# Strassen products for q, k and v in one phase, and attention that reads k and v from DRAM

## The chip, the core and the metric

The kernel runs on one core of one Trainium2 chip. The metric is device time in microseconds. Before the change three runs took 3925.47, 3927.17 and 3927.51 us; the median is 3927.17 us. The engines are TensorE (PE, with its weight loads listed apart as PEld), VectorE (DVE), ScalarE (ACT), GpSimd (POOL) and SyncE (SP), which here only issues DMAs.

## What is computed

A cross-attention block and a sparse feed-forward block, all in float32. There are 16 batches of 100 latent rows of 1024 numbers, and for each batch a context of 361 rows of 1024. There are 32 heads of 128 in 4 groups that share k and v.

```
x1  = x + xattn(layernorm(x), ctx, Wq, Wk, Wv, Wo)
out = x1 + ffn(layernorm(x1), c1_w, c2_w, w1, w2t)

xattn(latents, context):
    hidden = concat([context, latents], axis=1)      # 461 rows a batch
    q = latents @ Wq                                 # 32 heads of 128
    k = hidden @ Wk ; v = hidden @ Wv                # 4 groups of 128
    scores = q . k / sqrt(128)
    out = softmax(scores) . v
    return out @ Wo
```

Note that the context goes into k and v as it is, and the latents are normalised first.

## The kernel before

Every product is made to nearly float32 accuracy out of three matmuls. Each operand is split into a high part (ScalarE's copy into the type fp32r) and a low part (VectorE subtracts the high part from the original). `product` (line 21) then adds high x high, high x low and low x high for each chunk of 128 contraction rows; `PAIRS` lists the three. Its matmul is line 26, so several products of the kernel share that line and are told apart by their tiles.

The phases up to the first output projection are:

- `normalise` (line 45) reads x, normalises it and transposes it into `xt`, with its two parts.
- `project_queries` (line 203) runs over the 32 heads of Wq. For each head it makes 4 tiles of 400 columns, 24 matmuls each (8 chunks of three). It stores q to `q_scratch` in DRAM. Behind the heads it splits Wk and Wv into `wkv`, which stays in SBUF, and it saves `xt` to DRAM.
- `attend` (line 333) loops over the 16 batches. One batch has 4 groups of 800 query rows in tiles of 116 (7 tiles a group, 28 a batch). The tiles pass through a pipeline, written out by hand for each engine. In step i, PE makes the scores of tile i (`score`, three matmuls of 462 columns), then the piece of the weighing that is due (`weigh`, line 635), then the four transposes of tile i - 3 (`turn`, line 622). VectorE takes the row maximum, ScalarE the exponential and its sum, VectorE the reciprocal, GpSimd scales the probabilities (line 552), PE transposes them, ScalarE and VectorE make the two parts of `pt`. When half a group's columns (400) stand in `pt`, they are weighed with v in three pieces of four matmuls. GpSimd also splits q for the next group (lines 539 and 543).
- Between these steps PE also makes v of the same batch (line 599, six steps), transposes the context of the next batch (line 578) and makes the next batch's k (line 587). ScalarE and VectorE split each of the results (lines 690 and 722). These pieces are dealt to the steps by `v_work` and `k_work`.

A semaphore wait stands in front of each instruction that needs another engine's result, and each engine goes through its own list in order. So an instruction that waits holds back all that is behind it on its engine.

The rest (`project_out`, a second `normalise`, the gate, `hidden_layer`, a second `project_out`) isn't touched.

## Time and profile before

| what | value |
|---|---|
| median of three runs | 3927.17 us |
| the profiled execution, span of core 0 | 3928.4 us |
| PE busy | 3767.7 us, 96% |
| PE weight loads busy | 3331.3 us, 85% |
| VectorE busy | 1663.9 us, 42% |
| ScalarE busy | 1179.7 us, 30% |
| GpSimd busy | 534.1 us, 14% |
| mean granted clock of TensorE | 0.982 |
| last operation of attention ends | 2151.8 us |

The profile gives a span from the first to the last instruction; for this execution it has no other time. Busy time of PE is the time in which some matmul was under way. Matmuls overlap, so the mean duration of one is longer than the distance at which they follow each other; the distance is what counts, and it is read from counts in a stretch or from two start times. A number in square brackets behind a row is the idle time of the engine just ahead of it, with what ended it.

### The profile page before, as it was taken

The numbers are of one execution on the slowest core, as the hardware profiler recorded it, in microseconds if no ns is written. First come the engines' busy times: TensorE is split into PE (matmuls) and PEld (weight loads), VectorE is DVE, ScalarE is ACT, GpSimd is POOL, SyncE is SP. The second block draws the span as 40 slices with busy tenths as digits, with TensorE's granted clock in tenths as the row PEclk, the third lists the DMA queues.
The fourth block names the chain that finished last, engine by engine and source line by source line (L and its number), as shares of the span: only waits on it lengthen the run. The fifth ranks groups of instructions, "written<-read, shape, count | busy, mean of one in ns | idle before, by whom it ended". The sixth has DMA issues, their size and how long they took to land. (4 is left out here: it accounts for less than half of the span.)

```text
span 3928.4 us, 57189 instructions
## 1 busy us (share of the span) xinstructions
PE 3767.7 (96%) x19678; PEld 3331.3 (85%) x19678; DVE 1663.9 (42%) x2934; ACT 1179.7 (30%) x2353; POOL 534.1 (14%) x786
## 2 busy tenths in 40 slices
PE   6999998999999999999998999999699999899999
PEld 6999997888888888888887787787699999788787
DVE  4111112555555555555554432432565666332322
ACT  3111112444444444444444322322311111222321
POOL 0000000333333333333333100000000000000000
PEclk8999998999999999999999999999899999999999
DMA  4665554222222222222221644543211121444543
GB/s 120 125 126 95 78 80 108 59 67 57 57 57 63 59 57 57 61 61 57 57 57 53 183 123 118 182 123 100 85 69 68 56 74 61 135 129 128 173 124 102
DMA packets 469228, 357.91 MB, mean 91 GB/s; under 512 B 193328, under 2 KB 418608, under 8 KB 468144
## 3 DMA queue, kind: packets, MB, share of 16 engines
q1 hardware_dynamic: 463648, 330.03, 32.2%
q0 software_dynamic: 5520, 27.10, 1.9%
q8 instruction: 35, 0.57, 0.1%
q14 instruction: 25, 0.20, 0.0%
HBM read 255.49 MB, written 101.58 MB: 91 GB/s over the span
## 5 line engine op out<-in xcount | busy, mean ns | idle before, releaser
L1337 PE MATMUL wo_acc<-wo_w,wo_l 128*128 128x512 f32 (+1 forms) x2496 | 576.0, 393 | 23.2 <-DVE wo_l L1287 22.9
L1337 PEld LDWEIGHTS wo_acc<-wo_w,wo_l 128*128 128x128 f32 (+1 forms) x2496 | 461.8, 185 | 137.3 <-DVE wo_w L1311 23.1
L26 PE MATMUL q_acc<-xt,wq_parts 128*128 128x400 f32 x3072 | 560.6, 345 | 9.0 <-DVE wq_parts L307 9.0
L26 PEld LDWEIGHTS q_acc<-xt,wq_parts 128*128 128x128 f32 x3072 | 560.2, 188 | 9.2 <-issue 9.2
L1337 PE MATMUL w_acc<-w_w,w_l 128*128 128x512 f32 (+1 forms) x2184 | 503.6, 393 | 22.2 <-DVE w_l L1287 22.2
L26 PE MATMUL hid_acc<-x1t,hid_w 128*128 128x400 f32 x2688 | 508.7, 347 | 1.9 <-DVE hid_h L1100 1.4
L1337 PEld LDWEIGHTS w_acc<-w_w,w_l 128*128 128x128 f32 (+1 forms) x2184 | 405.1, 186 | 120.6 <-DVE w_w L1311 24.6
L26 PEld LDWEIGHTS hid_acc<-x1t,hid_w 128*128 128x128 f32 x2688 | 487.3, 189 | 2.6 <-issue 1.6
L552 POOL TENSOR_SCALAR probs<-probs,inverse 116x461 f32<-116x461 f32 (+1 forms) x448 | 293.4, 655 | 1025.9 <-DVE inverse L740 1025.4
L698 ACT ACTIVATE pt<-turned 128x464 fp32r<-128x464 f32 (+1 forms) x448 | 247.4, 552 | 582.0 <-PE turned L622 580.9
L732 DVE TENSOR_REDUCE negmax<-scores 116x1 f32<-116x461 f32 (+1 forms) x448 | 283.3, 632 | 311.4 <-PE scores L26 311.4
L587 PE MATMUL kvb<-hst,wkv 128*128 128x462 f32 x1536 | 387.4, 386 | 1.2 <-DVE hst L722 1.2
L599 PE MATMUL kvb<-wkv,hst 128*128 128x512 f32 (+1 forms) x1536 | 376.0, 397 | 0.0
L746 DVE TENSOR_TENSOR pt<-turned,pt 128x464 fp32r<-128x464 f32 (+1 forms) x448 | 283.0, 632 | 219.4 <-ACT pt L698 211.3
L26 PE MATMUL scores<-kt,q_parts 128*116 128x462 f32 (+1 forms) x1344 | 369.2, 383 | 2.3 <-DVE kt L722 1.5
L635 PE MATMUL outs<-pt,v 128*128 128x400 f32 (+1 forms) x1536 | 344.5, 346 | 7.6 <-DVE v L722 6.2
L599 PEld LDWEIGHTS kvb<-wkv,hst 128*128 128x128 f32 (+1 forms) x1536 | 269.9, 178 | 75.7
L705 ACT ACTIVATE probs<-scores,negmax 116x461 f32<-116x461 f32 (+1 forms) x448 | 288.4, 644 | 142.8 <-DVE negmax L732 140.7
L635 PEld LDWEIGHTS outs<-pt,v 128*128 128x128 f32 (+1 forms) x1536 | 283.4, 189 | 33.7 <-issue 11.8
L587 PEld LDWEIGHTS kvb<-hst,wkv 128*128 128x128 f32 x1536 | 275.5, 191 | 23.3 <-issue 1.5
L1287 DVE TENSOR_TENSOR wo_l<-wo_l_raw,wo_l 128x512 fp32r<-128x512 f32 (+1 forms) x208 | 139.3, 672 | 342.1 <-ACT wo_l L1260 342.1
L26 PEld LDWEIGHTS scores<-kt,q_parts 128*116 128x116 f32 (+1 forms) x1344 | 223.7, 178 | 39.9 <-issue 1.9
(98 smaller groups left out, 2926.7 us busy)
## 6 DMA issues: line engine op xcount, KB each, us to landing
wo_l_raw<-o_scratch SPq DMA_DIRECT2D x192, 256.0 KB, 2.8
w_l_raw<-h_scratch SPq DMA_DIRECT2D x168, 256.0 KB, 2.9
q_scratch<-q_stage SPq DMA_DIRECT2D x32, 800.0 KB, 8.2
q_raw<-q_scratch SPq DMA_DIRECT2D x64, 400.0 KB, 3.2
o_scratch<-o_stage SPq DMA_DIRECT2D x64, 400.0 KB, 3.9
h_scratch<-hid_h SPq DMA_DIRECT2D x28, 800.0 KB, 3.7
wq_raw<-in_L_xattn_Wq_dram SPq DMA_DIRECT2D x32, 512.0 KB, 8.1
ctx_raw<-in_ctx_dram SPq DMA_DIRECT2D x16, 1024.0 KB, 7.2
```

The costliest lines, as they stand in the source:

```text
L26: last = pe.matmul(out, left(a, c), right(b, c), start=(c == 0 and (a, b) == PAIRS[0]), stop=(c == chunks - 1 and (a, b) == PAIRS[-1]))
L552: pool.tensor_scalar(probs[:n, i % RB, :kv], probs[:n, i % RB, :kv], inverse[:n, i % RB:i % RB + 1], 1.0, ALU.mult, ALU.mult).then_inc(sca ...
L587: mm = pe.matmul(kvb[:, u % KB, :kvp], wkv[:, 0, a, c, g * P:(g + 1) * P], hst[:, e, c, :], start=(x == 0), stop=(x == products - 1))
L599: mm = pe.matmul(kvb[:n, k % KB, :], hst[:, a, c, at:at + n], wkv[:, 1, e, c, :], start=(x == 0), stop=(x == products - 1))
L635: mm = pe.matmul(outs[:, h, :half], v[:n, a, k, g * P:(g + 1) * P], pt[:n, e, k, h * half:(h + 1) * half], start=(x == 0), stop=(x == NC * ...
L698: act.activation(pt[:, 0, :, at:at + n], turned_tile(j, n), ACT.Copy).then_inc(pt_high, 1)
L705: act.activation(probs[:n, i % RB, :kv], scores[:n, i % SB, :kv], ACT.Exp, bias=negmax[:n, i % RB:i % RB + 1], accum_out=total[:n, i % RB: ...
L732: dve.tensor_reduce(negmax[:n, i % RB:i % RB + 1], scores[:n, i % SB, :kv], AX.X, ALU.max, negate=True).then_inc(s_max, 1)
L746: dve.tensor_tensor(pt[:, 1, :, at:at + n], turned_tile(j, n), pt[:, 0, :, at:at + n].bitcast(F32), ALU.subtract).then_inc(pt_low, 1)
L1287: dve.tensor_tensor(l[j % 2][:, 1, :, :rows], l_raw[j % 2][:, :, :rows], l[j % 2][:, 0, :, :rows].bitcast(F32), ALU.subtract).then_inc(l_l ...
L1337: last = pe.matmul(acc[p][:rows, :], l[j % 2][:, a, k, :rows], w[:, c, m * per + k, :], start=(m == 0 and k == 0 and (a, c) == PAIRS[0]), ...
```

## The change

`normalise` for x, `project_queries` and the k and v work inside `attend` are replaced by one function, `project`. It goes through ten sets of columns: eight of two batches of context (362 columns each, one of them padding), and two of eight batches of x (400 columns twice). For each set it goes through pairs of weight blocks: block n and the block half the heads away. A pair of weight blocks, a pair of column halves and the two halves of the 1024 contraction rows make a product of 2 x 2 blocks, and this is done by Strassen's scheme (in Winograd's form) with seven block products instead of eight. Each has 4 chunks of three matmuls. The sums of blocks that the scheme needs ahead are made by GpSimd (`sums_w` for every pair, `sums_x` and `last_x` for every set); ScalarE and VectorE split the seven results for each operand into parts; the sums behind the products are made out of PSUM by ScalarE (two copies) and VectorE (five). The tiles of the next set are transposed between the products of the present one. The parts of the next set's x operand (`high_x`, `low_x`) are made during the last pair of the set, each as soon as the product that reads the old one is done.

All of q, k and v are stored to DRAM. `attend` reads them from there: k comes as it is needed, v is transposed (line 877) since it is stored with its channels first. The tiles have 128 rows. Six fill 768 of a group's 800 rows, and the 32 rows that are left of each of the four groups make one tile more, the tail tile, the first of its batch. That gives 25 tiles a batch. Its 12 score matmuls take each group's k in turn, against a q that is zero elsewhere. GpSimd copies the tail's columns for group G to the end of `pt` (`bring_tail`, line 842) ahead of the second half's weighing. The halves have now 384 and 416 columns. A weighing now starts one step after the last transpose of its half (`s = j - step_of(...) - 1`). The score banks are three instead of two. Everything is unrolled: there are no hardware loops in either function.

On PE, in the last batch of before, around the end of a first half: `turned` are the transposed probabilities, `outs` the weighed sums. The first transpose here is of the half's last tile.

```order
L622 MATMUL turned<-ident,probs 128x116 [waits pt_low,scaled]
L622 MATMUL turned<-ident,probs 128x116 x3
L26 MATMUL scores<-kt,q_parts 116x462 [waits exped,q_split]
L26 MATMUL scores<-kt,q_parts 116x462 x2
L622 MATMUL turned<-ident,probs 128x116 [waits pt_low,scaled]
L622 MATMUL turned<-ident,probs 128x116 x3
L26 MATMUL scores<-kt,q_parts 116x462 [waits exped]
L26 MATMUL scores<-kt,q_parts 116x462 x2
L635 MATMUL outs<-pt,v 128x400 [waits o_out,pt_low]
L635 MATMUL outs<-pt,v 128x400 x3
```

After the change, in the first batch, at the end of a second half. The transpose of 128x128 is of the half's last tile.

```order
L26 MATMUL scores<-kt,q_parts 128x462 [waits exped]
L26 MATMUL scores<-kt,q_parts 128x462 x2
L925 MATMUL outs<-pt,v 128x384 x4
L906 MATMUL turned<-ident,probs 128x128 [waits pt_low,scaled]
L906 MATMUL turned<-ident,probs 128x128 x2
L906 MATMUL turned<-ident,probs 77x128
L26 MATMUL scores<-kt,q_parts 128x462 [waits exped]
L26 MATMUL scores<-kt,q_parts 128x462 x2
L925 MATMUL outs<-pt,v 128x416 [waits tail_in,pt_low]
L925 MATMUL outs<-pt,v 128x416 x3
```

One tile was transposed between the half's last tile and its weighing; now there is none, and the weighing waits on `tail_in` too.

On GpSimd, one group of before: the scaling of the probabilities with the pieces of q between.

```order
L552 TENSOR_SCALAR probs<-probs,inverse 116x461 [waits inverted] x2
L539 TENSOR_SCALAR q_parts<-q_raw 128x400 [waits q_landed1]
L552 TENSOR_SCALAR probs<-probs,inverse 116x461 [waits inverted]
L543 TENSOR_TENSOR q_parts<-q_raw,q_parts 128x400 [waits q_high]
L552 TENSOR_SCALAR probs<-probs,inverse 116x461 [waits inverted]
L539 TENSOR_SCALAR q_parts<-q_raw 128x400
L552 TENSOR_SCALAR probs<-probs,inverse 116x461 [waits inverted]
L543 TENSOR_TENSOR q_parts<-q_raw,q_parts 128x400 [waits q_high]
L552 TENSOR_SCALAR probs<-probs,inverse 116x461 [waits inverted]
L552 TENSOR_SCALAR probs<-probs,inverse 104x461 [waits inverted]
```

After the change, from the middle of group 0 of the first batch on: `kt` is the low part of the next batch's k, the COPY is `bring_tail`.

```order
L855 TENSOR_SCALAR probs<-probs,inverse 128x461 [waits inverted] x3
L812 TENSOR_SCALAR q_parts<-q_raw 128x384 [waits s_full,q_landed0]
L855 TENSOR_SCALAR probs<-probs,inverse 128x461 [waits inverted]
L812 TENSOR_SCALAR q_parts<-q_raw 128x384
L833 TENSOR_TENSOR kt<-k_raw,kt 128x462 [waits k_high]
L842 COPY pt<-pt_tail 128x8x32 [waits pt_low]
L855 TENSOR_SCALAR probs<-probs,inverse 128x461 [waits inverted]
L816 TENSOR_TENSOR q_parts<-q_raw,q_parts 128x384 [waits q_high]
L855 TENSOR_SCALAR probs<-probs,inverse 128x461 [waits inverted]
```

The low parts of k, which VectorE made before, and the copy of the tail's columns have come to GpSimd, and the copy stands behind a scaling, a piece of q and a part of k.

The diff, cut to its core:

```diff
-def project_queries(nc, sem, wq, kv_sources, wkv, xt, q_dram, xt_dram, scale, batches, rows, stage_free, saved):
+A, B, C, D = range(4)
+BANK = (A, B, A, D, B, C, D)
+def project(nc, sem, x, ctx, wq, wk, wv, ident, q_dram, k_dram, v_dram, scale):
...
+    sets = [("ctx", p) for p in range(NCTX)] + [("x", t) for t in range(batches // (2 * per))]
+    def pairs_of(s):
+        kv = [(kind, g) for kind in ("k", "v") for g in range(groups // 2)]
+        return kv if sets[s][0] == "ctx" else [("q", n) for n in range(heads // 2)] + kv
+    work = [(s, kind, n) for s in range(NS) for kind, n in pairs_of(s)]
+    NG = len(work)
+    opens = [min(g for g in range(NG) if work[g][0] == s) for s in range(NS)] + [NG]
...
+    def turn_slot(t):
+        s, k = tiles[t][0], t - of_set[tiles[t][0]][0]
+        if s == 0:
+            return -1
+        return 7 * opens[s - 1] + (2 + 2 * k if sets[s][0] == "ctx" else 3 + 2 * k if s == NCTX else 12 + 4 * k)
...
+        def w_from(G, i):
+            r = wr[G % 2]
+            return (r[:, 0, :half, :], sf[:, 1], r[:, 0, half:, :], sf[:, 0], sf[:, 2], r[:, 1, half:, :], sf[:, 3])[i]
...
+            def sums_w(G):
+                r = wr[G % 2]
+                pool.wait_ge(w_landed[G % 2], 32 * (G // 2 + 1))
+                if G:
+                    pool.wait_ge(s_made, 4 * G)
+                    pool.wait_ge(w_low, 7 * (G - 1) + 4)
+                pool.tensor_tensor(sf[:, 0], r[:, 1, :half, :], r[:, 1, half:, :], ALU.add).then_inc(s_made, 1)
+                pool.wait_ge(s_made, 4 * G + 1)
+                pool.tensor_tensor(sf[:, 1], sf[:, 0], r[:, 0, :half, :], ALU.subtract).then_inc(s_made, 1)
+                if G:
+                    pool.wait_ge(w_low, 7 * (G - 1) + 5)
+                pool.tensor_tensor(sf[:, 2], r[:, 0, :half, :], r[:, 1, :half, :], ALU.subtract).then_inc(s_made, 1)
+                if G:
+                    pool.wait_ge(w_low, 7 * (G - 1) + 7)
+                pool.wait_ge(s_made, 4 * G + 2)
+                pool.tensor_tensor(sf[:, 3], r[:, 0, half:, :], sf[:, 1], ALU.subtract).then_inc(s_made, 1)
+            def sums_x(s):
+                n = columns(s)
+                pool.wait_ge(xf_full, of_set[s][-1] + 1)
+                if s:
+                    pool.wait_ge(x_low, 7 * (s - 1) + 6)
+                pool.tensor_tensor(tf[:, 0, :, :n], xf[:, :half, 1, :n], xf[:, :half, 0, :n],
+                                   ALU.subtract).then_inc(t_made, 1)
+                pool.wait_ge(t_made, 4 * s + 1)
+                pool.tensor_tensor(tf[:, 1, :, :n], xf[:, half:, 1, :n], tf[:, 0, :, :n],
+                                   ALU.subtract).then_inc(t_made, 1)
+                pool.tensor_tensor(tf[:, 2, :, :n], xf[:, half:, 1, :n], xf[:, :half, 1, :n],
+                                   ALU.subtract).then_inc(t_made, 1)
+            def last_x(s):
+                n = columns(s)
+                pool.wait_ge(x_low, 7 * s + 2)
+                pool.tensor_tensor(tf[:, 1, :, :n], xf[:, half:, 0, :n], tf[:, 1, :, :n],
+                                   ALU.subtract).then_inc(t_made, 1)
...
+            for G in range(NG):
+                s = work[G][0]
+                if G + 1 < NG:
+                    sums_w(G + 1)
+                if s + 1 < NS:
+                    if G == ends[s] - 1:
+                        sums_x(s + 1)
+                    if G == ends[s]:
+                        last_x(s + 1)
...
+            for G in range(NG):
+                s = work[G][0]
+                n = columns(s)
+                for i in range(7):
+                    p = 7 * G + i
+                    pe.wait_ge(w_low, p + 1)
+                    if G == opens[s]:
+                        pe.wait_ge(x_low, 7 * s + i + 1)
+                    if i == 0 and G:
+                        pe.wait_ge(by_act, 2 * G)
+                    if i == 1 and G:
+                        pe.wait_ge(by_dve, 5 * (G - 1) + 2)
+                    if i == 2:
+                        pe.wait_ge(by_act, 2 * G + 1)
+                    if i == 3 and G:
+                        pe.wait_ge(by_dve, 5 * G)
+                    if i == 4:
+                        pe.wait_ge(by_dve, 5 * G + 1)
+                    if i == 6:
+                        pe.wait_ge(by_dve, 5 * G + 3)
+                    opened = i in (2, 4, 6)
+                    for c in range(half):
+                        for a, e in PAIRS:
+                            last = pe.matmul(bank[:, BANK[i], :n], wo[:, i, a, c, :], xo[:, i, e, c, :n],
+                                             start=(not opened and c == 0 and (a, e) == PAIRS[0]),
+                                             stop=(c == half - 1 and (a, e) == PAIRS[-1]),
+                                             skip_group_check=opened)
+                    last.then_inc(prod, 1)
+                    for t in turns[p]:
+                        turn(t)
...
+                for i in range(7):
+                    p = 7 * G + i
+                    if i == 1:
+                        dve.wait_ge(prod, p + 1)
+                        dve.wait_ge(by_act, 2 * G + 1)
+                        if G:
+                            dve.wait_ge(by_dve, 5 * G)
+                        add(G, u2, B, s1, n, f)
+                    if i == 4:
+                        dve.wait_ge(prod, p + 1)
+                        add(G, u3, B, s1, n, f)
+                        if G:
+                            dve.wait_ge(stored[3], 16 * G)
+                        dve.wait_ge(by_dve, 5 * G + 2)
+                        add(G, out[3], D, u3, n, f)
+                    if i == 5:
+                        dve.wait_ge(prod, p + 1)
+                        if G:
+                            dve.wait_ge(stored[2], 16 * G)
+                        add(G, out[2], C, u3, n, f)
+                    if i == 6:
+                        dve.wait_ge(prod, p + 1)
+                        if G:
+                            dve.wait_ge(stored[1], 16 * G)
+                        add(G, out[1], D, u2, n, f)
+                    if G + 1 < NG:
+                        low_w(G + 1, i)
+                    if G == ends[s] and s + 1 < NS:
+                        low_x(s + 1, i)
-def attend(nc, sem, ctx, xt_dram, q_dram, wkv, o_dram, ident, q_stored, xt_stored, o_free):
+def attend(nc, sem, q_dram, k_dram, v_dram, o_dram, ident, o_free):
...
+    TG = cols // P
+    body = TG * P
+    left = cols - body
+    split = body // 2
+    NT = 1 + groups * TG
+    N = batches * NT
+    NGR = batches * groups
+    SB, TB, OB, RB, LAG, PARTS = 3, 2, 2, 4, 3, 3
+    spans = ((0, split), (split, cols))
+    assert left * groups == P and NC * P <= 512
+    def place(I):
+        b, i = divmod(I, NT)
+        return (b, None, None) if i == 0 else (b, groups * b + (i - 1) // TG, (i - 1) % TG)
...
+    def pieces(j):
+        out = []
+        for G in range(max(0, groups * (j // NT) - 2), min(NGR, groups * (j // NT + 1))):
+            for h in range(2):
+                s = j - step_of(G, TG // 2 - 1 if h == 0 else TG - 1) - 1
+                if 0 <= s < PARTS:
+                    out.append((G, h, s))
+        return out
...
+            def low_k(b, g):
+                pool.wait_ge(k_high, groups * b + g + 1)
+                pool.tensor_tensor(kt[b % 2][:, 1, g], k_raw[:, g], kt[b % 2][:, 0, g].bitcast(F32),
+                                   ALU.subtract).then_inc(k_low, 1)
+            def bring_tail(G):
+                g = G % groups
+                pool.wait_ge(pt_low, (G // groups) * NT + 1)
+                if G:
+                    pool.wait_ge(o_full, 2 * G)
+                pool.tensor_copy(pt[:, :, :, body:], pt_tail[:, :, :, g * left:(g + 1) * left]).then_inc(tail_in, 1)
...
+            for I in range(N + LAG + 1):
+                if I < N:
+                    b, G, t = place(I)
+                    pool.wait_ge(inverted, I + 1)
+                    pool.tensor_scalar(probs[:, I % RB, :kv], probs[:, I % RB, :kv], inverse[:, I % RB:I % RB + 1],
+                                       1.0, ALU.mult, ALU.mult).then_inc(scaled, 1)
+                    if t is not None and 0 <= t < 4 and G + 1 < NGR:
+                        split_q(G + 1, *divmod(t, 2))
+                    if I % NT in (8, 10, 12, 14) and b + 1 < batches:
+                        low_k(b + 1, (I % NT - 8) // 2)
+                    if I % NT == 18 and b + 1 < batches:
+                        split_tail(b + 1)
+                j = I - LAG - 1
+                if j >= 0 and place(j)[2] == 3:
+                    bring_tail(place(j)[1])
...
+            def weigh(G, h, s):
+                b, g = divmod(G, groups)
+                lo, hi = spans[h]
+                for x in range(NC * len(PAIRS) * s // PARTS, NC * len(PAIRS) * (s + 1) // PARTS):
+                    k, (a, e) = x // len(PAIRS), PAIRS[x % len(PAIRS)]
+                    n = kv_chunks[k][1]
+                    if x == 0:
+                        pe.wait_ge(pt_low, step_of(G, TG // 2 - 1 if h == 0 else TG - 1) + 1)
+                        if h == 1:
+                            pe.wait_ge(tail_in, G + 1)
+                        if h == 0 and g == 0:
+                            pe.wait_ge(v_low, NC * (b + 1))
+                        if G:
+                            pe.wait_ge(o_act if h == 0 else o_dve, G)
+                    last = pe.matmul(outs[:, h, :hi - lo], v[b % 2][:n, a, k, g * P:(g + 1) * P], pt[:n, e, k, lo:hi],
...
+            for I in range(LAST):
+                if I < N:
+                    score(I)
+                j = I - LAG
+                for G, h, s in pieces(j) if j >= 0 else ():
+                    weigh(G, h, s)
+                if 0 <= j < N:
+                    turn(j)
+                b, i = divmod(I, NT)
+                if i in (8, 11, 14, 17) and b + 1 < batches:
+                    turn_v(b + 1, (i - 8) // 3)
...
-                normalise(nc, sem, "ln1", x.rearrange("b r n -> (b r) n"), xt, ident)
-                project_queries(nc, sem, wq, (wk, wv), wkv, xt, q_dram, xt_dram, float(d) ** -0.5, batches, rows,
-                                q_stored, xt_stored)
-            attend(nc, sem, ctx, xt_dram, q_dram, wkv, o_dram, ident, q_stored, xt_stored, o_stored)
+        project(nc, sem, x, ctx, wq, wk, wv, ident, q_dram, k_dram, v_dram, float(d) ** -0.5)
+        attend(nc, sem, q_dram, k_dram, v_dram, o_dram, ident, o_stored)
```

## Rows read from the trace of the kernel before

**Rows 1.** Windows by stage: from:to, length, busy us (count), PEclk, DMA share, GB/s
```profile
0.00:55.80 55.80, 21.12 (x104) 19.77 (x105) 36.60 (x81) 30.98 (x33) 1.10 (x8) 0.76 0.40 137
55.80:616.40 560.60, 560.60 (x3072) 560.23 (x3072) 83.75 (x102) 72.45 (x103) 4.43 (x8) 1.00 0.55 104
616.40:663.20 46.80, 28.58 (x122) 24.10 (x121) 7.41 (x13) 6.95 (x13) 4.93 (x6) 0.74 0.51 125
663.20:2078.10 1414.90, 1396.12 (x7620) 1204.68 (x7621) 737.78 (x1619) 623.93 (x1514) 455.66 (x660) 1.00 0.22 58
2078.10:2151.80 73.70, 70.59 (x389) 59.69 (x387) 42.45 (x97) 36.17 (x89) 27.31 (x40) 1.00 0.13 34
2151.80:3928.40 1776.60, 1690.73 (x8374) 1462.79 (x8374) 755.92 (x1023) 409.18 (x603) 40.69 (x64) 0.98 0.37 114
```

**Rows 2.** Windows, 100 us of the query phase
```profile
200.00:300.00 100.00, 100.00 (x552) 100.00 (x551) 12.50 (x17) 11.37 (x17) 1.60 (x3) 1.00 0.66 128
```

**Rows 3.** Timeline, last batch: start us, us, engine, line ... [idle <-releaser]
```profile
2113.57 0.56 PE L622 MATMUL turned<-ident,probs 116*128 116x116 f32 x4
2113.89 0.86 PE L26 MATMUL scores<-kt,q_parts 128*116 128x462 f32 x3
2114.16 0.56 ACT L698 ACTIVATE pt<-turned 128x464 fp32r<-128x464 f32 x1 [0.63 <-PE turned L622]
2114.59 0.90 PE L635 MATMUL outs<-pt,v 128*128 128x400 f32 x4
2114.75 0.64 DVE L746 TENSOR_TENSOR pt<-turned,pt 128x464 fp32r<-128x464 f32 x1 [0.61 <-ACT pt L698]
2115.33 0.56 PE L622 MATMUL turned<-ident,probs 116*128 116x116 f32 x4
```

**Rows 4.** Timeline, the end of the last batch
```profile
2141.72 0.86 PE L26 MATMUL scores<-kt,q_parts 128*104 128x462 f32 x3
2143.14 0.96 PE L622 MATMUL turned<-ident,probs 116*128 116x116 f32 x8
2143.74 0.56 ACT L698 ACTIVATE pt<-turned 128x464 fp32r<-128x464 f32 x1 [0.57 <-PE turned L622]
2144.04 0.65 POOL L552 TENSOR_SCALAR probs<-probs,inverse 116x461 f32<-116x461 f32 x1 [1.11 <-DVE inverse L740]
2144.33 0.64 DVE L746 TENSOR_TENSOR pt<-turned,pt 128x464 fp32r<-128x464 f32 x1 [0.49 <-ACT pt L698]
2145.03 1.00 PE L635 MATMUL outs<-pt,v 128*128 128x400 f32 x4 [0.93 <-DVE pt L746]
```

**Rows 5.** Groups by line and form: xcount | busy us, mean ns | idle
```profile
L543 POOL TENSOR_TENSOR q_parts<-q_raw,q_parts 128x400 fp32r<-128x400 f32 x128 | 134.5, 1051 | 0.2
L539 POOL TENSOR_SCALAR q_parts<-q_raw 128x400 fp32r<-128x400 f32 x128 | 67.3, 526 | 14.5 <-DMA q_raw<-q_scratch 14.5
L1287 DVE TENSOR_TENSOR wo_l<-wo_l_raw,wo_l 128x512 fp32r<-128x512 f32 x192 | 132.5, 692 | 308.7 <-ACT wo_l L1260 308.7
L307 DVE TENSOR_TENSOR wq_parts<-wq_raw,wq_parts 128x1024 fp32r<-128x1024 f32 x32 | 39.2, 1226 | 22.9 <-ACT wq_parts L278 22.9
L1100 DVE SCALAR_TENSOR_TENSOR hid_h<-hid_acc,hid_mask_t 128x400 f32<-128x400 f32 x112 | 59.0, 568 | 132.3 <-ACT hid_mask_t L1044 121.6 <-PE hid_acc L26 5.5 <-issue 5.2
```

**Rows 6.** Timeline of PE in the hidden layer
```profile
3060.84 0.60 PE L954 MATMUL turn<-ident,hid_raw 128*128 128x128 f32 x4
3061.20 0.72 PE L965 MATMUL gate<-c2s,zs 80*128 x4
3061.76 0.53 PE L26 MATMUL hid_acc<-x1t,hid_w 128*128 128x400 f32 x2
```

**Rows 7.** DMA queue, 400 to 500 us: packets, MB, share of 16 engines
```profile
q1 hardware_dynamic: 17250, 7.41, 47.3%
```

**Rows 8.** Timeline, the first transposes of attention
```profile
630.32 1.44 PE L578 MATMUL kvb<-ident,ctx_raw 128*128 128x128 f32 x6 [13.90 <-DMA ctx_raw<-in_ctx_dram]
```

**Rows 9.** Windows, 20 us of the first output projection
```profile
2180.00:2200.00 20.00, 16.38 (x65) 12.55 (x64) 11.74 (x13) 8.84 (x11) 0.00 (x0) 0.93 0.81 259
```

939 lines of the change are left out of this document (505 added, 434 removed).

## Prediction

> **What bounds the kernel now.** I read five views. First the stretches by stage [rows 1]: TensorE (PE) is busy for 560.6 of 560.6 us in the query phase, for 1396 of 1415 us in the attention loop and for 70.6 of 73.7 us in its last batch; nothing else passes 740 us in the loop. So up to 2151.8 us the end is set by the number of matmuls and by what each one takes. Second, the rate inside one line [rows 2]: 552 matmuls of 400 columns in 100 us, 181.2 ns each. Third, the last batch in order of time [rows 3, 4], the only stretch of before in which attention runs without k or v products between its steps: what an attention step takes there, and how long a tile needs from its transpose to the moment when it can be weighed. Fourth, the costs of single operations [rows 5, 6]. Fifth, the DMA packets [rows 7] and the crossing into attention [rows 8]. The change ends ahead of the first output projection, so I compare when attention ends: 2151.8 us before. The 1776.6 us behind it stay as they are.
>
> **The new first phase.** Its matmuls: seven products of 12 for each pair of weight blocks, 84. Eight context sets of 4 pairs with 362 columns are 2688; two x sets of 20 pairs with 400 columns are 3360. Before, the same work was 3072 of 400, 1536 of 462 and 1536 of 512 columns.
>
> A matmul of 400 columns is in the trace, 181.2 ns [rows 2]. One of 362 is not. If it costs no less it is 181; in proportion it is 164. Four gate matmuls of 256 columns take 0.56 us, 140 ns each [rows 6], and the line from there to 400 gives 170. I take 168; the ends are 2604 x 4 ns = 10 us less and 2604 x 13 ns = 34 us more. The Trainium skill (TensorE: Matmul & The Clock Gate, Back-to-back issue gap) gives N/2.4 + 2.5 ns for an isolated matmul, 153 ns for 362 columns, and says that this counts high for large N. For 400 columns it would be 169, and the trace does not agree: 181.2. By it the term below would be 39 us smaller.
>
> - Start: nothing is normalised ahead, but six context tiles, the first weights and all seven parts of both operands have to be made before the first pair can end. Three 512 KB tiles by about 10 us, 1 MB of weights by 17, the other tiles by 24. GpSimd then makes the sums of x: 2.63 ns an element L543 takes 1051 ns for 400, [rows 5], so 3.8 us for each of 4 x 362 elements; the second is ready at 32. ScalarE rounds (1.4) and VectorE subtracts (1.7), the part for the second product stands at 35, and then VectorE's pairs of operations go at 2.4 us to about 46. ScalarE evacuates product 0 only behind its list of 14, and product 2 waits for that. The pair ends at about 60 us, with the clock at its lower level at first as in the first of [rows 1]. Between 50 and 75.
> - The other 31 context pairs: 2604 x 168 ns = 437.5 us. The 40 x pairs: 3360 x 181.2 ns = 609 us.
> - Transposes: 42 context tiles of 8 at 90 ns (four in 0.36 us, [rows 6]) = 30 us; 16 x tiles of 8 at 80 ns (four in 0.32, [rows 3]) = 10 us.
> - Changes of set, 9. In the last pair of a set VectorE has, beside its seven weight parts (692 ns each, [rows 5] L1287) and five sums (568, L1100), the seven parts of the next operand. Between L1287 (512 elements, 692 ns) and L307 (1024, 1226 ns) an element costs 1.04 ns, so 1448 elements take 1.67 us. I let each hide 0.08 us behind the one before (an estimate). Its order up to the third sum is 4 x (0.61 + 1.59) + three sums = 10.3 us and starts 3.3 us into the pair, with waits 14.3; PE wants that sum after six products, at 12.2. So PE waits 2.1 us, a little more with 400 columns: 9 x 2.2 = 20 us. The next pair takes up the rest of the backlog.
> - In an ordinary pair I find no wait. VectorE has 7.7 of 15.2 us. The weights: 2048 + 2048 packets a pair of q. In [rows 7] 47.3% of 100 us of 16 queues carried 17250 packets, 44 ns each, so 11.2 of 15.2 us. They are asked for 1.4 us into the pair, land about 12 us into it, and are wanted at 17.5.
> - GpSimd's sums (four of 1.35 us a pair, four of 3.8 us a set) now run beside VectorE's subtractions of two SBUF operands. The trace has no such pair of operations side by side: L543 runs beside a subtraction out of PSUM, and both keep their times. If that holds the cost is 0. If the two exclude each other, a context set has 28 x 0.65 + 7 x 1.6 + 16 x 1.35 + 15.2 = 66 us of them against 61 us of PE, and bunched at the end of the set: sums_x delays the third sum in the last pair but one by about 7 us, last_x and the weight sums by 6 in the last, 9 x 13 = 117 us. I take 25, near the end for which there is a row.
>
> Sum: 60 + 437.5 + 609 + 40 + 20 + 25 = 1191.5 us.
>
> **Crossing into attention.** Before, 13.9 us between the last q matmul and the first transpose [rows 8]. Now the stores are waited for (4 us), the block changes (2), k lands after 4.5 more, q, v and the tail rows by 16; GpSimd then splits the tail, the first q (3 us) and three of four k (3.6) before the first score: 23 us. Between 15 and 30.
>
> **Attention.** A step of the last batch takes 1.76 us [rows 3]: three score matmuls 0.70, four of the output 0.74, four transposes 0.32. Of 1.76 us ScalarE waits 0.63 and VectorE 0.61 [rows 3], so neither is the bound when the k and v work is gone. A batch of 25 tiles: 24 x 0.705 for scores, 2.8 for the tail tile with its 12, 96 x 0.1825 = 17.5 for outputs, 116 transposes at 0.088 = 10.2. That is 47.4 us, 758 for 16. The tiles are fewer, but the matmuls of scores (84) and outputs (96) are as many as before: 25 for 28 saves PE only transposes.
>
> Two waits come with it.
> - First half of a group. Before, one tile is transposed between the half's last tile and its weighing; now none, as the two pieces on PE show. The drain of before has just that distance once [rows 4]: transpose 2143.14, ScalarE's copy 2143.74, VectorE's subtraction 2144.33, PE goes on at 2145.03, having waited 0.93. From transpose to weighing 1.89 us, 2.0 with 128 columns; PE gets there after 0.355 + 0.705 = 1.06. It waits 0.95 us, three times a batch (the fourth time the tail tile's long score lies between).
> - Second half. It waits for the same, and for GpSimd to bring the tail's 32 columns (L842). That copy stands behind the scaling of the tile two steps before the weighing. Scaling ends 2.97 us after the next tile's score begins (2141.72 to 2144.04 + 0.65, [rows 4]). Behind it stand a piece of q (0.52, L539), in two of the four groups a subtraction of k (L833, 462 x 2.63 = 1.2 us) and the copy itself (0.4). So 4.0 or 5.2 us after that score, where PE wants it after 1.78 + 0.70 = 2.5. Waits of 1.5 and 2.7 us, two each, 8.4 us a batch.
>
> Queued behind the waiting weighing on PE are the transposes, and behind these ScalarE's copy and exponential; they have 0.6 us a step to spare, so the wait costs its own length and no more. 2.9 + 8.4 = 11.3 us a batch, 180 us for 16. Ends: 45 us (only the first-half waits, should GpSimd be earlier than the drain shows) and 230. With 3 us to fill and 5 to drain: 758 + 180 + 8 = 946.
>
> **Sum.** 1191.5 + 23 + 946 = 2160.5 us against 2151.8, 8.7 us longer. The profiled execution spans 3928.4 us, 1.2 above the median of 3927.2, and has no time of its own beside its span. So 3937.1 there and **3936 us** as a median, 0.2% slower: 190 us of matmuls saved in the products, given back in waits of attention, at set changes and at the crossing.
>
> **Rivals.**
> 1. The attention waits are mostly hidden, because GpSimd runs earlier once VectorE has no k and v parts to make. For it: its busy share is 37% in the last batch. Against: its lag is set by VectorE and ScalarE, not by its own load [rows 4]. Price: 135 of 180 us go, 3801; with the port term gone too, 3776. Faster. It decides once the tail copy ends less than 2.5 us after the score of the step before the weighing. Chance 0.20.
> 2. GpSimd and VectorE exclude each other in the first phase, price up to 117 instead of 25, on average 75: 3986, and up to 4028. Nothing in the trace speaks for or against. Chance 0.28. The Trainium skill (SBUF — State Buffer, on the shared port pair) states it as an exclusive lock for the whole instruction between a VectorE operation with two SBUF inputs and a GpSimd one that reads SBUF; no row here shows it.
> 3. TensorE's clock drops in attention. In [rows 9], with a gap of 3.6 us and 82% busy, the granted clock was 0.93, between its levels of 1.2 and 2.4 GHz; attention would be 80% busy with gaps up to 2.7. At 0.93, 758 us become 815: 3993. Against: the last batch keeps 1.00, with smaller gaps. Chance 0.10.
> 4. The forecast, 0.42, with its own range of 3895 to 3985 (matmul of 362 columns, start, port, waits).
>
> About 0.2% (8 us) is what a measurement of this kernel tells from no change. Faster: the first rival and a third of the forecast's lower part, 0.35. Same: 0.13. Slower: 0.52. The range 3800 to 4015 takes in rivals 1 to 3 except their ends.
>
> **What would show it.** A stretch of the x pairs at 181 ns a matmul with PE always busy, and of context pairs at 168; before L925 with 416 columns idle time released by POOL, about 1.5 and 2.7 us, 64 times, and before L925 with 384 columns about 0.95, released by VectorE; attention batches of 58.7 us. Were they 48 us, the first rival holds. GpSimd's sums longer than 1.35 us, or VectorE's parts well over 0.69 beside them, would show the second; a granted clock under 1.00 in attention the third. The forecast is wrong if PE in the x pairs waits for weights or for DMA, since 40 pairs repeat it.

## The result and the profile after

The changed kernel takes 4101.4 us (median of four runs, 4097.0 to 4105.8) against 3926.3 (3925.3 to 3927.5): ratio 1.0445, interval 1.0433 to 1.0458. That is 4.5% slower; 3936 was forecast, and the range, up to 4015, did not hold it. Its profiled execution spans 4095.4 us, 167.0 longer than that of before.

The windows of the kernel after, cut at its stages (columns as in [rows 1]: busy time and count per engine, granted clock, DMA share, GB/s), answer to [rows 1]:

```profile
76.08:521.00 444.92, 386.42 (x2259) 382.37 (x2258) 342.04 (x325) 207.10 (x291) 243.33 (x120) 0.91 0.45 132
521.00:1325.30 804.30, 742.17 (x4054) 733.97 (x4052) 521.75 (x734) 300.33 (x485) 298.14 (x192) 0.96 0.44 115
1325.30:1346.80 21.50, 4.14 (x17) 2.94 (x17) 3.56 (x5) 3.81 (x7) 10.45 (x13) 0.61 0.42 139
1346.80:2321.50 974.70, 832.06 (x4722) 741.41 (x4720) 593.80 (x1325) 580.43 (x1386) 544.77 (x806) 0.96 0.30 83
2321.50:4095.40 1773.90, 1689.03 (x8374) 1461.19 (x8374) 755.71 (x1022) 409.62 (x603) 40.86 (x64) 0.98 0.37 114
```

The first phase ends at 1325.3 us (forecast 1191.5), the crossing takes 21.5 (23), attention 974.7 (946), the rest 1773.9 (1776.6 before). So 134 of the missed 161 us lie in the first phase, and both stretches show a granted clock under 1.00.

One context set in PE's own timeline (start, duration, line, operands, count, idle time before it and its releaser):

```profile
127.40 1.04 PE L441 MATMUL pr_tp<-ident,pr_raw 128*128 128x128 f32 x8
152.23 14.20 PE L470 MATMUL pr_bank<-pr_xo,pr_wp 128*128 128x362 f32 x84
170.53 16.76 PE L470 MATMUL pr_bank<-pr_xo,pr_wp 128*128 128x362 f32 x84 [4.11 <-DVE pr_out L609]
192.71 10.04 PE L470 MATMUL pr_bank<-pr_xo,pr_wp 128*128 128x362 f32 x48 [5.42 <-DVE pr_out L609]
202.58 1.04 PE L441 MATMUL pr_tp<-ident,pr_raw 128*128 128x128 f32 x8
```

The set takes 75.2 us (127.40 to 202.58); its matmuls and transposes are worth 61.4. PE waits twice for VectorE's third sum, 9.5 us; and the 84 matmuls behind the first wait take 16.8 us where 84 without a wait took 14.2. The granted clock was 1.00 in the stretch ahead (152.23 to 166.43) and 0.56 from 170.53 to 177.00, so nearly all of that time at the lower of its two levels; behind the second wait it was 0.62 from 192.71 to 198.00. The undisturbed 14.20 / 84 = 169 ns is the forecast's 168.

What holds VectorE, in the timelines of VectorE and of GpSimd over the same moment:

```profile
182.33 1.66 DVE L571 TENSOR_TENSOR pr_xo<-pr_tf,pr_xo 128x1448 fp32r<-128x1448 f32 x1
184.51 4.79 DVE L571 TENSOR_TENSOR pr_xo<-pr_xf,pr_xo 128x1448 fp32r<-128x1448 f32 x1
189.82 1.66 DVE L571 TENSOR_TENSOR pr_xo<-pr_tf,pr_xo 128x1448 fp32r<-128x1448 f32 x1
192.03 0.54 DVE L609 SCALAR_TENSOR_TENSOR pr_out<-pr_bank,pr_u 128x362 f32<-128x362 f32 x1
```

```profile
184.07 3.71 POOL L414 TENSOR_TENSOR pr_tf<-pr_xf,pr_tf 128x1448 f32<-128x1448 f32 x1 [6.76 <-DVE pr_xo L571]
190.07 2.53 POOL L387 TENSOR_TENSOR pr_sf<-pr_wr 128x512 f32<-128x512 f32 x1 [2.30 <-DVE pr_wp L565]
```

The same subtraction takes 1.66 us alone and 4.79 beside GpSimd's last_x. GpSimd's ends at 187.78, and VectorE's ends 1.52 us later: it did nearly its whole work behind it. It also goes the other way. At 189.82 VectorE starts first and keeps its 1.66 us, and GpSimd's sum of the weights beside it takes 2.53 where it takes 1.26 to 1.28 alone. The two took turns. The Trainium skill (SBUF — State Buffer, SBUF: two separate sides) says that whichever of such a pair starts first has the shared port for its whole instruction; this trace agrees in both orders. The groups of VectorE's weight parts in this kernel (count, busy us, mean ns, idle before):

```profile
L565 DVE TENSOR_TENSOR pr_wp<-pr_sf,pr_wp 128x512 fp32r<-128x512 f32 x288 | 274.7, 954 | 87.0 <-ACT pr_wp L488 79.3
L565 DVE TENSOR_TENSOR pr_wp<-pr_wr,pr_wp 128x512 fp32r<-128x512 f32 x216 | 251.7, 1165 | 202.8 <-ACT pr_wp L488 202.5
```

Alone they would take 692 ns, as L1287 in [rows 5].

The set of x tiles, PE's timeline, has a wait that the forecast did not have:

```profile
593.47 0.91 PE L441 MATMUL pr_tp<-ident,pr_raw 100*128 100x100 f32 x8 [1.92 <-ACT pr_raw L519]
```

L519 normalises a tile; 29.3 us in all are idle ahead of transposes for it. VectorE's factors stand behind a product, a rounding and a subtraction, then come six small operations and ScalarE's 1.24 us, with two products of time for all of it.

Attention, PE's timeline, then GpSimd's at the same place (they answer to [rows 3, 4]):

```profile
1792.06 0.87 PE L26 MATMUL scores<-kt,q_parts 128*128 128x462 f32 x3
1794.86 0.99 PE L925 MATMUL outs<-pt,v 128*128 128x416 f32 x4 [1.93 <-issue]
1801.80 0.97 PE L925 MATMUL outs<-pt,v 128*128 128x384 f32 x4 [0.79 <-DVE pt L1027]
1809.74 1.00 PE L925 MATMUL outs<-pt,v 128*128 128x416 f32 x4 [1.93 <-issue]
1810.93 1.25 PE L26 MATMUL scores<-kt,q_parts 128*128 128x462 f32 x3
1811.98 1.59 PE L925 MATMUL outs<-pt,v 128*128 128x416 f32 x4
1825.09 0.99 PE L925 MATMUL outs<-pt,v 128*128 128x416 f32 x4 [1.24 <-DVE pt L1027]
```

```profile
1792.15 0.66 POOL L855 TENSOR_SCALAR probs<-probs,inverse 128x461 f32<-128x461 f32 x1 [0.63 <-DVE inverse L1023]
1792.77 0.52 POOL L812 TENSOR_SCALAR q_parts<-q_raw 128x384 fp32r<-128x384 f32 x1
1793.25 1.17 POOL L833 TENSOR_TENSOR kt<-k_raw,kt 128x462 fp32r<-128x462 f32 x1
1794.36 0.40 POOL L842 CAST pt<-pt_tail 128x256 fp32r<-128x256 f32 x1
1824.59 0.40 POOL L842 CAST pt<-pt_tail 128x256 fp32r<-128x256 f32 x1
```

The queue is the forecast one: scaling, a piece of q, a piece of k, the tail copy, and PE goes on 0.1 us behind it ("issue" stands for that wait). The wait of 1.24 us ends 0.1 us behind the tail copy too (1824.59 and 0.40), though its row names VectorE. Waits of 1.93, 1.24 and 0.79 us were forecast at 2.7, 1.5 and 0.95. Not forecast is what follows the one at 1809.74: three score matmuls in 1.25 us instead of 0.87, four output matmuls in 1.59 instead of about 0.86, at a granted clock of 0.57 from 1811 to 1815 us.

### The profile page after: what moved, and what is told of

Its sections match the earlier page's. It is cut to its first block and busy times, and to the rows that moved or that the text cites. A ratio compares the mean times of both kernels' runs of the same rounds, so it can differ in the third digit from the quotient of the medians.

```text
span 4095.4 us, 56421 instructions
## 1 busy us (share of the span) xinstructions
PE 3700.4 (90%) x19670; PEld 3366.4 (82%) x19670; DVE 2257.6 (55%) x3445; ACT 1535.7 (37%) x2812; POOL 1173.7 (29%) x1220
## 5 line engine op out<-in xcount | busy, mean ns | idle before, releaser
L470 PE MATMUL pr_bank<-pr_xo,pr_wp 128*128 128x400 f32 (+1 forms) x6048 | 1128.4, 349 | 110.9 <-DVE pr_out L609 86.0
L470 PEld LDWEIGHTS pr_bank<-pr_xo,pr_wp 128*128 128x128 f32 x6048 | 1104.5, 197 | 117.9 <-issue 112.1
L925 PE MATMUL outs<-pt,v 128*128 128x384 f32 (+3 forms) x1536 | 366.6, 362 | 125.5 <-DVE pt L1027 67.7
L1027 DVE TENSOR_TENSOR pt<-turned,pt 128x512 fp32r<-128x512 f32 x384 | 265.3, 691 | 292.1 <-ACT pt L977 292.0
L855 POOL TENSOR_SCALAR probs<-probs,inverse 128x461 f32<-128x461 f32 x400 | 262.6, 656 | 422.6 <-DVE inverse L1023 419.1
L26 PE MATMUL scores<-kt,q_parts 128*128 128x462 f32 x1152 | 349.6, 413 | 16.5 <-POOL q_parts L816 16.2
L565 DVE TENSOR_TENSOR pr_wp<-pr_wr,pr_wp 128x512 fp32r<-128x512 f32 x216 | 251.7, 1165 | 202.8 <-ACT pr_wp L488 202.5
L977 ACT ACTIVATE pt<-turned 128x512 fp32r<-128x512 f32 x384 | 229.9, 599 | 350.2 <-PE turned L906 350.1
L565 DVE TENSOR_TENSOR pr_wp<-pr_sf,pr_wp 128x512 fp32r<-128x512 f32 x288 | 274.7, 954 | 87.0 <-ACT pr_wp L488 79.3
L1016 DVE TENSOR_REDUCE negmax<-scores 128x1 f32<-128x461 f32 x400 | 251.2, 628 | 22.1 <-PE scores L890 20.7
```

What stands on the lines that cost most here:

```text
L26: last = pe.matmul(out, left(a, c), right(b, c), start=(c == 0 and (a, b) == PAIRS[0]), stop=(c == chunks - 1 and (a, b) == PAIRS[-1]))
L470: last = pe.matmul(bank[:, BANK[i], :n], wo[:, i, a, c, :], xo[:, i, e, c, :n], start=(not opened and c == 0 and (a, e) == PAIRS[0]), stop ...
L565: dve.tensor_tensor(wo[:, i, 1], w_from(G, i), wo[:, i, 0].bitcast(F32), ALU.subtract).then_inc(w_low, 1)
L855: pool.tensor_scalar(probs[:, I % RB, :kv], probs[:, I % RB, :kv], inverse[:, I % RB:I % RB + 1], 1.0, ALU.mult, ALU.mult).then_inc(scaled, 1)
L925: last = pe.matmul(outs[:, h, :hi - lo], v[b % 2][:n, a, k, g * P:(g + 1) * P], pt[:n, e, k, lo:hi], start=(x == 0), stop=(x == NC * len(P ...
L977: act.activation(pt_of(j, 0), turned[:, j % TB, :, :], ACT.Copy).then_inc(pt_high, 1)
```

## Experiments

Theory P: GpSimd's sums and VectorE's subtractions take turns, VectorE falls behind at each change of set, and PE waits. Its rival V: VectorE's own list is too long there. Beside these: the normalising chain (N), the tail copy (T) and the weighing (W) in attention. One execution each, set against the 4101.4 of after, but for the last run. The four runs of after lie 8.7 us apart, so differences of 4 or 5 us are not told from none.

### All of GpSimd's sums narrow

```
- tensor_tensor(sf[:, 0], r[:, 1, :half, :], ...)   # and the 7 other sums
+ tensor_tensor(sf[:, 0, :, :8], r[:, 1, :half, :8], ...)
```

> GpSimd's sums of the weights (from the second pair on) and of x (but for the first context and the first x set) are made on 8 columns of 128 and 362 or 400; the rest of the operands is left as it was, so q, k and v are not the reference's. VectorE, ScalarE and TensorE keep all their instructions. Theory P (GpSimd and a VectorE subtraction with two SBUF operands take turns, and the backlog of VectorE makes PE wait at each change of set): L565 returns from 0.95 and 1.17 us to 0.69, a context set takes 62 to 64 us instead of 75.15, the first phase ends 95 to 110 us earlier, the time is about 4000. Rival V (VectorE's own list is too long at a change, GpSimd is only the neighbour): a context set stays at 73 to 75, time 4090 to 4105.

Measured 3987.3, 114 less. PE's timeline, and VectorE's weight parts in the groups:

```profile
134.47 28.15 PE L471 MATMUL pr_bank<-pr_xo,pr_wp 128*128 128x362 f32 x168
164.97 9.75 PE L471 MATMUL pr_bank<-pr_xo,pr_wp 128*128 128x362 f32 x48 [2.34 <-DVE pr_out L610]
229.88 9.74 PE L471 MATMUL pr_bank<-pr_xo,pr_wp 128*128 128x362 f32 x48 [2.34 <-DVE pr_out L610]
```

```profile
L566 DVE TENSOR_TENSOR pr_wp<-pr_sf,pr_wp 128x512 fp32r<-128x512 f32 x288 | 205.6, 714 | 101.4 <-ACT pr_wp L489 91.2
L566 DVE TENSOR_TENSOR pr_wp<-pr_wr,pr_wp 128x512 fp32r<-128x512 f32 x216 | 153.4, 710 | 231.3 <-ACT pr_wp L489 228.1
```

A set takes 64.9 us, the last wait but one is gone and the last is 2.34 us: the 2.2 that the forecast gave VectorE's own list. P holds, V falls: VectorE has every instruction it had. The phase ends at 1215.5 us, 109.8 earlier. By the groups of PE, 65.7 us of this are waits ahead of products (110.9 to 45.2), 33.9 are busy time of the same matmuls (1128.4 to 1094.5) and 9.6 are waits for the x tiles (29.3 to 19.7). It is rather a lower bound, since the sums of the first x set were left whole, and at that change PE still waits 7.31 us (7.21 in the kernel after).

One more rival is that the narrow sums help because they are ready sooner. The groups of ScalarE speak against it: it waits 17.6 us for the weights' sums in the kernel after and 52.5 here. What went is VectorE's own busy time, 526 to 359 us for the weight parts.

### Only the sums of the weights narrow

The edit is that of the run before for `sums_w` alone.

> Only GpSimd's sums of the weights are narrowed to 8 columns (computed values as in the run with all sums narrow); the four sums of x a set stay whole. Theory P: of the 21 us of GpSimd's work in the last two pairs of a set 11 go; a context set takes 67 to 70 us, the time is 4040 to 4065. Should the sums of x alone make the waits: 73 to 75 and 4085 to 4100. Rival V: no change.

Measured 4059.0, 42 less, and sets of 72.6, 73.6 and 72.9 us (the 73.6 from 158.91 to 232.54, from product 6 of one set to that of the next). So the time came as expected and the set did not, for which 67 to 70 were expected: in the context sets the sums of x carry about 8 of the 10.3 us. The weights' sums gave the rest of their 42 elsewhere: 12 us are waits for L519, which fall from 29.3 to 17.3, and 7 us come in the first pair, whose last two products start at 49.97 instead of 56.89. There the kernel after has this wait for VectorE's sum, which is 1.38 us here:

```profile
51.69 3.96 PE L470 MATMUL pr_bank<-pr_xo,pr_wp 128*128 128x362 f32 x12 [5.36 <-DVE pr_u L609]
```

### The sums of x on VectorE

```
- if G == ends[s] - 1: sums_x(s + 1)      # GpSimd
- if G == ends[s]: last_x(s + 1)
+ if G == ends[s] - 1 and i >= 4: sum_x(s + 1, i - 4)   # VectorE
+ if G == ends[s] and i == 1: sum_x(s + 1, 3)
```

> The four sums of x a set are made by VectorE (1.7 us each) instead of GpSimd (3.8 us each); the sums of the weights stay with GpSimd. Nothing is left out. If the two engines take turns, 15.2 us of blocked VectorE become 6.7 us of work: the wait of the last pair but one (4.1) goes mostly, that of the last shrinks by 2; time 4040 to 4070. Rival V, no exclusion: VectorE has 6.7 us more to do at each change, the time rises by 9 x 2 to 6 us, 4120 or more.

Measured 4054.5, 47 less, though VectorE has 6.7 us more to do a set. PE's timeline:

```profile
173.55 5.77 PE L467 MATMUL pr_bank<-pr_xo,pr_wp 128*128 128x362 f32 x24 [2.24 <-DVE pr_u L606]
182.87 8.22 PE L467 MATMUL pr_bank<-pr_xo,pr_wp 128*128 128x362 f32 x48 [3.55 <-DVE pr_out L606]
```

The waits are 2.24 and 3.55 in place of 4.11 and 5.42, the set 69.1 us; its neighbours take 70.1 to 71.1, and in two of the first five the last wait is 5.09. That the time falls at all is what V excludes.

### The parts of x three products later

```
- if G == ends[s]: high_x(s + 1, i)       # and low_x
+ x = i - 3 (from the last pair of a set into the next one)
```

> ScalarE rounds and VectorE subtracts each part of the next set's x three products later than now (both in lists and in step); no work is removed. Theory P with backlog: PE's wait before product 6 comes from the low parts of x that stand ahead of the sums in VectorE's list, made long by GpSimd; with one such part ahead in place of four the wait of the last pair (5.4 us) goes, that of the last but one (4.1) stays: 9 x 5.4 and 2 us of clock each, 4101 - 50 to 65: 4036 to 4051. Rival: the backlog then stops product 4 to 6 of the next pair instead, time over 4085.

Measured 4130.4, 29 more. PE's timeline:

```profile
192.43 6.21 PE L470 MATMUL pr_bank<-pr_xo,pr_wp 128*128 128x362 f32 x36 [0.99 <-DVE pr_out L610]
201.17 2.21 PE L470 MATMUL pr_bank<-pr_xo,pr_wp 128*128 128x362 f32 x12 [2.53 <-issue]
205.54 2.21 PE L470 MATMUL pr_bank<-pr_xo,pr_wp 128*128 128x362 f32 x12 [1.29 <-issue]
209.32 2.24 PE L470 MATMUL pr_bank<-pr_xo,pr_wp 128*128 128x362 f32 x12 [1.56 <-DVE pr_u L610]
217.10 3.62 PE L470 MATMUL pr_bank<-pr_xo,pr_wp 128*128 128x362 f32 x12 [2.68 <-DVE pr_out L610]
```

The 5.42 became 0.99, as expected, and then four waits of 8.1 us together, which the rival said. Order alone does not take work off VectorE.

### Both

> Both: the parts of x three products later, the sums of x on VectorE. Theory P: hardly a wait of set changes is left, a context set takes 63 to 66 us instead of 75.15; time 3990 to 4015. Rival: the gains overlap, no better than the better of the two by over 10 us.

Measured 4050.2: 4 us below the sums of x alone, no difference in single runs. A miss; the rival holds.

### GpSimd with one operand

```
- tensor_tensor(to, one, two, op)
+ tensor_scalar(to, one, 1.0, 1.0, mult, mult)
```

> GpSimd's sums (but for the first pair's and the sums of the first context and first x set) become a copy of their first operand, elements and places unchanged, so q, k and v are not the reference's. VectorE is untouched. If any GpSimd operation out of SBUF takes turns with VectorE's subtraction of two SBUF operands, VectorE's subtractions stay far over 0.69 us where they meet it, but GpSimd is busy for half as long (1.34 ns an element in place of 2.63): L565 at 0.8 to 0.95 in the mean, time 4030 to 4060. If only two operands on both sides collide: L565 at 0.69 to 0.72 in the mean, and the time is that of the run with narrow sums, 3985 to 3995.

Measured 4009.3, between the two expectations. VectorE's and GpSimd's timeline, and the groups:

```profile
232.00 1.78 POOL L384 TENSOR_SCALAR pr_tf<-pr_xf 128x1448 f32<-128x1448 f32 x1 [6.58 <-DVE pr_xo L576]
232.43 2.87 DVE L576 TENSOR_TENSOR pr_xo<-pr_xf,pr_xo 128x1448 fp32r<-128x1448 f32 x1
252.96 0.62 POOL L384 TENSOR_SCALAR pr_sf<-pr_wr 128x512 f32<-128x512 f32 x1 [6.30 <-DVE pr_wp L570]
```

```profile
L570 DVE TENSOR_TENSOR pr_wp<-pr_sf,pr_wp 128x512 fp32r<-128x512 f32 x288 | 209.6, 728 | 102.6 <-ACT pr_wp L493 92.8
L570 DVE TENSOR_TENSOR pr_wp<-pr_wr,pr_wp 128x512 fp32r<-128x512 f32 x216 | 159.4, 738 | 225.9 <-ACT pr_wp L493 224.1
```

GpSimd's ends at 233.78, VectorE's 1.52 later: a GpSimd operation with one operand blocks as well. It costs less because it is short. The means stay near 0.73, lower than I had worked out; why is not shown. Some of the blocking falls on GpSimd, whose copies of 512 elements take 0.62 us in the median and up to 2.18.

### The normalising chain earlier

```
- turn_slot(t) - 3 == p: moments_of(t)   # - 2 factors, root; - 1 norm
+ turn_slot(t) - 4 == p: moments_of(t)   # - 3 factors, root; - 2 norm
```

> Moments, factors, root and normalisation of each x tile one product earlier in the lists of VectorE and ScalarE. Theory N: the chain of factors starts only behind a product and two subtractions and takes 5 us where PE gives it two products, 4.4 us; a product earlier the 34 us that PE waits for L519 fall under 8, time 4070 to 4080. Rival: what is late is the tile's DMA or ScalarE itself, then the waits stay over 25 us and the time over 4093.

Measured 4091.0, 10 less where 20 to 30 were expected. The groups of PE (the first has ACT pr_raw L519 29.3 in the kernel after, and the second 110.9):

```profile
L441 PE MATMUL pr_tp<-ident,pr_raw 128*128 128x128 f32 (+2 forms) x512 | 66.0, 276 | 10.5 <-DMA pr_raw<-in_ctx_dram 10.5
L470 PE MATMUL pr_bank<-pr_xo,pr_wp 128*128 128x400 f32 (+1 forms) x6048 | 1128.9, 349 | 132.0 <-DVE pr_out L609 94.9 <-DVE pr_xo L571 14.3 <-ACT pr_s L546 11.8
```

The waits for L519 are gone, and 21 of the 29 us stand in front of products now: VectorE and ScalarE are full in that set. The term was hidden behind another.

### The tail copy earlier

```
- if j >= 0 and place(j)[2] == 3: bring_tail(...)
+ if j >= 0 and place(j)[2] == 1: bring_tail(...)
```

> GpSimd brings the tail's columns two tiles earlier (behind the scaling of the tile with place 5 in place of the one with place 7 of the group's count). Theory T: the second-half waits (2.1 us, two a batch, and 1.4, two a batch) fall to the 0.95 that VectorE's subtraction leaves; 3.2 us a batch, 51 in all, and a little of the clock: time 4035 to 4055. Rival: the waits for the tail only cover waits of the same length for VectorE's subtraction: time over 4085.

Measured 4012.5, 89 less, more than the 45 to 65 expected. The windows of its attention:

```profile
1346.80:2236.00 889.20, 796.17 (x4710) 708.62 (x4710) 592.33 (x1323) 577.79 (x1385) 545.78 (x806) 1.00 0.32 90
```

PE idles 93.0 us instead of 142.6, the expected 50; and the same matmuls are busy for 796.2 us instead of 832.1, at a granted clock of 1.00. With the waits over 1 us the lower clock goes too, for 36 us.

### The weighing later

```
- s = j - step_of(...) - 1      # tail copy at place 3
+ s = j - step_of(...) - 2      # tail copy at place 2
```

> Each half of a group is weighed one tile later on PE, and GpSimd brings the tail's columns one tile earlier; the first phase is as in the kernel after. Moving the tail copy alone gave 4012.5 and left 76.4 us of waits for VectorE's subtraction (L1027) ahead of the output matmuls. Theory W: these waits go too (under 10 us left), and the clock rises with them: 4012.5 - 76 - 10 to 25 for the clock, 3900 to 3930. Rival: the waits move to the scores or transposes behind, because ScalarE and VectorE then are late: time over 3970.

Measured 3931.1, 170 less. Windows of its attention, and two groups of PE:

```profile
1346.00:2152.50 806.50, 778.91 (x4717) 718.82 (x4715) 589.84 (x1325) 579.81 (x1385) 545.26 (x806) 1.00 0.35 99
```

```profile
L925 PE MATMUL outs<-pt,v 128*128 128x384 f32 (+3 forms) x1536 | 342.7, 345 | 0.9 <-DVE pt L1027 0.9
L26 PE MATMUL scores<-kt,q_parts 128*128 128x462 f32 x1152 | 336.8, 401 | 26.2 <-POOL q_parts L816 25.9 <-ACT probs L983 0.2
```

Attention without these waits takes 806.5 us, and what is left idle waits for the next q. The matmuls are busy for 17.3 us less than in the run before (778.9 for 796.2), and both runs show a granted clock of 1.00: so waits add to the busy time by something beside the clock. What, is not shown; that a matmul next to a wait has no neighbour to overlap with would do it.

### Towards a faster kernel

The kernel before took 3933.5 us beside the first four of these runs and 3925.6 beside the last. All five keep the later weighing, split q one to two tiles earlier, and have the sums of x on VectorE. From the second on the weights' sums are there too:

```
+ sum_w(G + 1, k) behind low_w(G + 1, i): {0: (0, 1), 1: (2,), 3: (3,)}
```

> The later weighing (3931.1 alone), the sums of x on VectorE (4101 to 4054.5 alone), and in attention GpSimd splits the next q one to two tiles earlier and k's low parts in other tiles. The first two lie in different phases and should add: 3931 - 47 = 3884; the 26 us that PE waits for q_parts L816 go by the new order: 3858 to 3865. If GpSimd's step with two pieces of q is late for the scaling, new waits for probs L855 come and it stays over 3875.

Measured 3849.1, below the expectation: the gains of the two phases add.

> As the run before in this call, and the sums of the weights on VectorE too; GpSimd is idle in the first phase. Theory P: a sum costs the pair of engines 1.35 us on GpSimd and 0.69 on VectorE, whose free share is taken in either case; the low parts L562 return to 0.69 us; a context set 64 to 68 us; 20 to 40 us below the run before: 3820 to 3845. Rival V (GpSimd's sums cost VectorE nothing while it waits anyway): 2.8 us more work for VectorE in each pair, the waits at set changes grow, 10 us or more above the run before.

Measured 3843.9, 5 us less for the expected 20 to 40, not clear of noise. The low parts are back at 0.70 us, yet a context set takes 69.7 to 70.8 us, as in the run before (70.0 to 70.1): waits of 2.24 and 3.57 or 5.1 us have become 0.77 and 6.3, and the one of 6.3 us in the last pair is VectorE's own list. Here V has its share.

> As all sums on VectorE with the later weighing, and moments, root, factors and normalisation of the x tiles one product earlier. Alone in the kernel after this took 29 us of waits for L519 away and gave 10 us, since VectorE was full in that set. If VectorE's fullness came from GpSimd, now 15 to 25 us below the run before; if from its own list, 0 to 12.

Measured 3839.4, 4.5 less: in the range for a VectorE filled by its own list, and not clear of noise.

> As all sums on VectorE with the later weighing, and the parts of the next x two products later, the transposes of the set after one product later. Three products later alone lost 29 us; the new waits stood at the next pair's products 3 to 6, behind fills that wait for the last part of x. Theory: with the fills moved too and less work on VectorE, the later parts win 10 to 25 us against the run with all sums on VectorE. Rival: the backlog is a sum of work and only moves: within 8 us of it or above.

Measured 3832.5, 11 less, a set 68.3 us: with room on VectorE, order pays a little.

> The version to keep: the later weighing, GpSimd's new order in attention, all sums on VectorE, the parts of x two products and the fills one product later, and the normalising chain of the x tiles one product earlier. Without the last part 3832.5 in one run; it alone gave 10 us in the kernel after and 4.5 with all sums on VectorE, where the set of x tiles was bound by VectorE. Expected 3824 to 3832, ratio to before 0.972 to 0.977.

Measured in five rounds: 3824.0 us (3818.6 to 3826.6) against 3925.6; ratio 0.9737, interval 0.9724 to 0.9750. PE's groups and a window of its attention:

```profile
L464 PE MATMUL pr_bank<-pr_xo,pr_wp 128*128 128x400 f32 (+1 forms) x6048 | 1109.1, 345 | 80.0 <-DVE pr_out L604 62.2 <-DVE pr_xo L566 14.8 <-DVE pr_u L604 2.2
```

```profile
1270.00:2100.00 830.00, 808.36 (x4877) 749.13 (x4878) 613.14 (x1355) 601.90 (x1417) 548.12 (x809) 0.98 0.40 113
```

So a kernel with the seven-for-eight products is 2.6% faster than before, once what they cost VectorE, GpSimd and the drain of a group is arranged; no run tells what the products alone give. 62 us of waits for VectorE's sums are still there.

## Why the prediction was wrong

The row that the port term leans on, in the kernel before, beside VectorE's L746 at 2114.75 in [rows 3]:

```profile
2114.96 1.04 POOL L543 TENSOR_TENSOR q_parts<-q_raw,q_parts 128x400 fp32r<-128x400 f32 x1
```

- **Right.** The context matmul (169 ns for 168), the x pairs, which never wait for weights or a DMA (551 matmuls in 100 us, as in [rows 2]; those of the first x set do wait for tiles of the second), the crossing (21.5 for 23), the rest (1773.9 for 1776.6), and the 2.2 us per change of VectorE's own list (2.34 without GpSimd). The start fits by luck: the first pair ended at 61.0 us, forecast 60, but 54.6 with the narrow sums, so 6 us of it come with GpSimd's sums, which the forecast had not put there.
- **The step that failed: the port term, "I take 25, near the end for which there is a row".** It is at least 110 us (1325.3 to 1215.5). The row of that end is L543 beside a subtraction out of PSUM (above). Both keep their times, but VectorE has one SBUF operand there; after too, L1027 beside GpSimd keeps 691 ns. It says nothing of two SBUF operands. The weight went to the nearest row although it was not of the same kind. This is 85 us of the 161. That 110 lies close to the upper end of 117 is in part luck: the 117 were waits alone, 13 us a change, and a change lost 7.2 us of waits (9.5 to 2.34). Waits ahead of products are 66 us of the 110; the other 44 are the longer busy time behind them and the waits for the x tiles.
- **The clock, rival 3.** Its price was 57 us. Attention's matmuls were busy for 832.1 us against 778.9 with the waits away, 53 us; 36 of them went as the granted clock rose from 0.96 to 1.00, and 17 at 1.00. In the first phase it adds to each change: 16.8 and 10.0 us behind the waits of one set, where 14.2 and 8.2 are the undisturbed times, 4.4 us. The argument against it, the last batch at 1.00, rests on a stretch without such gaps.
- **A missing term.** The chain of x tiles: 29 us of waits, of which 10 could be had back alone. I had counted the tiles' transposes and not who makes them ready; its six small operations and ScalarE's pass stood in the diff.
- **The attention waits.** 180 us forecast, 142.6 us of idle time in all. Mechanism and places were right, each wait 0.2 to 0.8 us shorter; 16 us of it are waits for the next q, not forecast. The other work is 779 for 758. With the 53 us: 779 + 143 + 53 = 975, forecast 946. So attention came within 29 us in part by luck: its waits were forecast 45 us too long (188 with fill and drain, for 143), against 53 and 21 us that were missing.
- **Rivals taken as alternatives.** Two and three were each given as a way for the whole kernel, with a chance, but they happen in different stages and both came. With 110 for 25 and 53 for 0, and 20 for the chain (the rest of its 29 is in the 110), the sum of 2160.5 becomes 2318; attention ended at 2321.5. That is no full account: 29 us more of the first phase are left over, and nearly as much was forecast too high in attention.

What stays open: why the clock is lower behind some waits and not behind others of the same length (behind 3.55 us 48 matmuls took 8.22, behind 3.60 they took 9.73, both with the sums of x on VectorE). This was not taken apart.

## What to carry to other kernels

Work given to an idle GpSimd is not free where VectorE subtracts two SBUF operands: count both in one list, and try it on VectorE when that does it in half the time: the sums of x gained 47 us there, those of the weights nothing clear. Waits of PE in a steady loop can cost more than themselves, since behind many of them the clock was lower (rows above, though not behind each); moving the consumer one step away from its producers' drain, with the tail copy one tile earlier, gave 170 us, and the copy two tiles earlier alone 89. Rivals that act in different stages add up: price them together. A row supports a term only if it shows the same kind of operands.
